# A convolution, router and experts kernel: tiles 2 and 3 on shared blocks in float32, routes ahead of rows in steps 2 to 11

## The reference

```python
out = lax.conv_general_dilated(x, weight, window_strides=(1,), padding=[(4, 4)],
                               feature_group_count=4)
y = out + einsum('nd,od->no', cond, c_weight)[:, :, None] + bias[None, :, None]
base_out = einsum('btd,od->bto', y, base_W) + base_b
probs = softmax(einsum('btd,nd->btn', y, router_W) + router_b)     # 15 routes
topk_p, topk_i = top_k(probs, 8)
w = einsum('btk,btke->bte', topk_p, onehot(expert_map[topk_i]))    # 8 experts
h = einsum('btd,erd->bter', y, A)                                  # rank 16
x = x + base_out + einsum('bter,eor->bto', h * w[..., None], B) * 2.0
```

## Time and profile before

| what | us |
|---|---|
| median of 3 runs | 185.14 |
| lowest, highest | 184.20, 185.57 |
| the profiled execution | 184.44 |
| its span in the profile | 182.6 |
| TensorE busy | 178.4 |

### The profile page before, as it was taken

How to read it: one execution, slowest core, us unless ns; L and a number is a source line. 1 busy time by engine, 2 the same in 40 slices (tenths; PEclk the granted TensorE clock), 3 DMA queues, 4 the chain that set the end, 5 groups by cost and what they waited for, 6 DMA issues and landing times.

```text
span 182.6 us, 3930 instructions
## 1 busy us (share of the span) xinstructions
PE 178.4 (98%) x1236; PEld 171.1 (94%) x1236; DVE 150.8 (83%) x509; ACT 81.2 (44%) x247; POOL 139.8 (77%) x139
## 2 busy tenths in 40 slices
PE   7999999999999999999999999999999999999993
PEld 3687999999999999999999999999999999999992
DVE  0597888898888889888888988889898889978673
ACT  3648743354544434454443445454344444422320
POOL 2118999999888898888889888888988887885620
PEclk9999999999999999999999999999999999999999
DMA  6999751757475553646565454656445721233304
GB/s 172 348 388 340 252 178 14 243 199 204 152 233 174 173 181 124 178 152 230 159 198 174 135 170 154 228 178 210 175 106 201 230 78 63 97 115 115 118 0 172
DMA packets 17876, 32.01 MB, mean 175 GB/s; under 512 B 1984, under 2 KB 3136, under 8 KB 17856
## 3 DMA queue, kind: packets, MB, share of 16 engines
q1 hardware_dynamic: 17424, 31.40, 53.1%
q10 hardware_dynamic: 432, 0.36, 0.6%
HBM read 23.36 MB, written 8.39 MB: 174 GB/s over the span
## 4 chain that ended last, share of the span: by engine, by line
PE 96%; DVE 2%; issue 0%; POOL 0%; DVEq 0%; POOLq 0%
PE wide_ps L606 62%; PE wide_ps L648 12%; PE conv_banks L592 11%; PE edge_bank L592 3%; PE conv_banks L606 2%; PE odd_bank L635 2%; PE wide_ps L554 2%; PE conv_banks L663 1%; PE conv_banks L565 1%; PE conv_banks L563 1%; DVE xr L966 1%; DVE y L856 0%; DVE y_rows L774 0%; PE edge_bank L621 0%; DVE y_hi L891 0%
## 5 line engine op out<-in xcount | busy, mean ns | idle before, releaser
L606 PE MATMUL wide_ps<-wide_hi,y_hi 128*128 128x400 f32 (+1 forms) x248 | 66.0, 326 | 0.1
L606 PE MATMUL wide_ps<-wide_hi,y_lo 128*128 128x400 f32 (+1 forms) x248 | 62.6, 313 | 0.0
L606 PE MATMUL wide_ps<-wide_lo,y_hi 128*128 128x400 f32 (+1 forms) x248 | 62.5, 313 | 0.0
L486 POOL TENSOR_TENSOR terms_lo<-terms,terms_hi 128x512 fp32r<-128x512 f32 x28 | 36.3, 1298 | 18.4 <-ACT terms_hi L385 18.4
L606 PEld LDWEIGHTS wide_ps<-wide_hi,y_hi 128*128 128x128 f32 x248 | 44.0, 188 | 2.5 <-issue 0.5
L606 PEld LDWEIGHTS wide_ps<-wide_lo,y_hi 128*128 128x128 f32 x248 | 45.9, 188 | 0.0
L606 PEld LDWEIGHTS wide_ps<-wide_hi,y_lo 128*128 128x128 f32 x248 | 45.9, 188 | 0.0
L504 POOL TENSOR_TENSOR y_lo<-y,y_hi 128x512 fp32r<-128x512 f32 x31 | 40.3, 1299 | 5.7 <-ACT y_hi L400 5.7
L481 POOL TENSOR_TENSOR xr<-xr,base_b_sb 128x512 f32<-128x512 f32 x32 | 41.7, 1302 | 0.0
L407 ACT ACTIVATE hw_hi<-odd_bank 128x128 fp32r<-128x128 f32 x31 | 8.6, 278 | 54.3 <-PE odd_bank L635 54.3
L768 DVE TENSOR_TENSOR xr<-wide_ps,xr 128x512 f32<-128x512 f32 x30 | 20.7, 691 | 5.2 <-PE wide_ps L648 3.8
(11 more groups left out here) (90 smaller groups left out, 308.4 us busy)
## 6 DMA issues: line engine op xcount, KB each, us to landing
xr<-x_rows SPq DMA_DIRECT2D x32, 256.0 KB, 3.6
out<-xr SPq DMA_DIRECT2D x31, 256.0 KB, 3.2
terms<-x_units SPq DMA_DIRECT2D x28, 256.0 KB, 2.9
...
```

The costliest lines, as they stand in the source:

```text
L486: nc.gpsimd.tensor_tensor(terms_lo[i % 2][:, :, :, :], terms[i][:, :, :, :], terms_hi[i % 2][:, :, :, :].bitcast(F32), ALU.subtract)\
L606: mm = nc.tensor.matmul(sums_of(t, k)[:, b, 0:columns[1] - columns[0]], a[k % 2][:, r, :], w[:, r, columns[0]:columns[1]], start=r == 0 an ...
```

## The change

- Tiles 2 and 3 use the shared blocks too, in float32 and without splitting (`conv_whole`): three matmuls of 256 columns for tile 2 with its edges, two for tile 3. Their differences are made by GpSimd (tile 2 and the edges, behind all of `wide_lo`, ahead of `conv_low(1)`) and by VectorE (tile 3). Their data are `first_terms` and `first_edges` in place of `x_in2` and `x_in3`; 12 weight matrices are loaded instead of 14, in another order, and the last of them earlier.
- The condition's sums of groups 1 and 2 stand together ahead of tile 0's sums, that of group 3 between their first two pieces; the sums of tile 0 take their pieces in another order.
- In steps 2 to 11 VectorE does only the first two additions of the rows, then `hw_low`, `choose` and `best`, then the edges (`reach`, split off from `condition`), and `difference` and `turn` at the end. ScalarE has `y_high` behind `hw_high`. From step 12 (`LATE`) the order is the old one.
- TensorE waits for the rows of the tile ahead only before the edge part of a convolution.
- At step 0 GpSimd does `bias_rows` ahead of `edge_low`, at step 1 ahead of `terms_low`.

The diff, cut to what changes an order or an amount of work:

```diff
-W_OWN, W_REACH = (1, 2, 5, 6), (0, 3, 4, 7)
-W_SUM, W_QUARTERS = (8, 9, 11, 12), (10, 13)
-W_ALL = 14
+W_OWN, W_REACH, W_SUM, W_QUARTERS = (1, 2, 4, 7), (0, 3), (9, 10, 5, 8), (11, 6)
+W_ALL = 12
...
-            load_x(2)
+            load_first_terms(0)
             sync.wait_ge(wide_in[0], 16)
+            sync.dma_start(first_edges[:, :, :, :], x_edges[0]).then_inc(first_edges_in, 16)
+            load_conv(4)
+            sync.wait_ge(wide_in[1], 16)
             load_conv(3)
-            load_x(3)
+            load_first_terms(1)
...
-            bias_condition(range(1, 2), 2)
+            bias_condition(range(1, GROUPS), 3)
             conv_high(1)
             y_high(1, 1, 2)
             odd_up(START, 0)
             exponentials(0, 0)
-            bias_condition(range(2, GROUPS), 3)
...
-                if up_to_tile(t, TILES - 2):
+                if from_tile(t, LATE) and up_to_tile(t, TILES - 2):
                     y_high(t + 1, k + 1)
                 if t == TILES - 1:
                     exponentials(t, k)
                 hw_high(t - 1, k - 1)
+                if not from_tile(t, LATE):
+                    y_high(t + 1, k + 1)
...
             conv_low(0)
+            pool.wait_ge(wide_lo_ready, RUNS)
+            pool.wait_ge(first_terms_in[0], 16)
+            nc.gpsimd.tensor_tensor(first_terms[0][:, 0, :, :], first_terms[0][:, 0, :, :],
+                                    first_terms[0][:, 1, :, :], ALU.subtract)\
+                .then_inc(first_difference[0], 1)
+            pool.wait_ge(first_edges_in, 16)
+            nc.gpsimd.tensor_tensor(first_edges[:, 0, :, :], first_edges[:, 0, :, :],
+                                    first_edges[:, 1, :, :], ALU.subtract)\
+                .then_inc(first_edge_ready, 1)
             conv_low(1)
             y_low(1, 1, 2)
...
-                    edge_low(p + 2, k // 2)
                     pool.wait_ge(base_b_in, 16)
                     bias_rows(t, k)
+                    edge_low(p + 2, k // 2)
                     y_low(t + 2, k + 2)
                     return
                 if t == 1:
+                    bias_rows(t, k)
                     terms_low(t + 4, k)
-                    bias_rows(t, k)
...
-                if t == START:
-                    pe.wait_ge(y_rows_ready, t - 1)
-                    pe.wait_ge(cond_biased, GROUPS)
-                elif h == 0:
-                    pe.wait_ge(y_rows_ready, t)
-                else:
-                    pe.wait_ge(y_rows_ready, t - 1)
+                pe.wait_ge(y_rows_ready, t - 1)
                 if h == 0:
                     parts.append((edge_ps, S_QUARTERS[g // 2], edge_hi, edge_lo))
                 if t < 2 * START and h == 0:
                     pe.wait_ge(conv_lo_ready, 2 + g // 2 * 2)
                 for n, (sums, j, hi, lo) in enumerate(parts):
                     if n == 2:
+                        pe.wait_ge(y_rows_ready, t)
                         pe.wait_ge(edge_lo_ready, p - START // 2 + 1)
...
-            def conv_later(t):
+            cond_sums(range(1, GROUPS - 1), 2)
+            def conv_whole(t):
+                i, h = t - FIRST, t % 2
                 pe.wait_ge(y_rows_ready, t - 1)
-                pe.wait_ge(conv_w_in[2], 16)
-                pe.wait_ge(x_loaded[t], 16)
-                conv_first(t)
+                pe.wait_ge(conv_w_in[2 + i], 16)
+                pe.wait_ge(first_terms_in[i], 16)
+                nc.tensor.matmul(conv_ps[:, h, 0, :, :], conv_sb[:, W_SUM[t], :],
+                                 first_terms[i][:, 1, :, :], start=True, stop=True)
+                pe.wait_ge(first_difference[i], 1)
+                mm = nc.tensor.matmul(conv_ps[:, h, 1, :, :], conv_sb[:, W_OWN[t], :],
+                                      first_terms[i][:, 0, :, :], start=True, stop=True)
+                if h == 0:
+                    pe.wait_ge(cond_biased, GROUPS)
+                    pe.wait_ge(first_edge_ready, 1)
+                    mm = nc.tensor.matmul(edge_ps, conv_sb[:, W_QUARTERS[t // 2], :],
+                                          first_edges[:, 0, :, :], start=True, stop=True)
+                mm.then_inc(conv_done, 1)
             def first_step():
                 runs = range(RUNS)
-                pe.wait_ge(y_hi_first, 1)
-                for r in runs:
+                def high(r):
                     pe.wait_ge(wide_hi_ready, r + 1)
                     linear(0, 0, (r,), products=(HIGH,))
-                    if r == 1:
-                        pe.wait_ge(y_lo_first, 1)
-                        linear(0, 0, range(2), products=(Y_REST,))
-                    elif r > 1:
-                        linear(0, 0, (r,), products=(Y_REST,), last=(RUNS - 1, W_REST))
-                for r in runs[:RUNS // 2]:
+                def y_rest(r):
+                    linear(0, 0, (r,), products=(Y_REST,))
+                def w_rest(r):
                     pe.wait_ge(wide_lo_ready, r + 1)
                     linear(0, 0, (r,), products=(W_REST,))
-                cond_sums(range(2, GROUPS), 2)
+                pe.wait_ge(y_hi_first, 1)
+                high(0)
+                cond_sums(range(GROUPS - 1, GROUPS), 2)
+                high(1)
+                pe.wait_ge(y_lo_first, 1)
+                y_rest(0)
+                y_rest(1)
+                high(2)
+                y_rest(2)
+                w_rest(0)
+                high(3)
+                linear(0, 0, (3,), products=(Y_REST,), last=(RUNS - 1, W_REST))
+                w_rest(1)
+                w_rest(2)
                 pe.wait_ge(wide_lo_ready, RUNS)
                 for bank, done in ((FRONT_BANK, front_done), (NEXT_BANK, linear_done)):
-                    linear(0, 0, runs[RUNS // 2:], (bank,), (W_REST,), (RUNS - 1, W_REST))\
+                    linear(0, 0, runs[RUNS - 1:], (bank,), (W_REST,), (RUNS - 1, W_REST))\
                         .then_inc(done, 1)
-                conv_later(2)
+                conv_whole(2)
...
+            def reach(t, g):
+                h = g % 2
+                shared = 1 - h
+                rows = y_rows[h]
+                reached = slice(EDGE, P) if h == 0 else slice(0, EDGE)
+                dve.wait_ge(own_ready, t - FIRST + 1)
                 nc.vector.tensor_tensor(rows[reached, :, shared, :], edge_ps[reached],
                                         rows[reached, :, shared, :], ALU.add)\
                     .then_inc(y_rows_ready, 1)
...
-            difference(START, 0)
             dve.wait_ge(top_ready, 1)
             mark(0, 0)
+            dve.wait_ge(first_terms_in[1], 16)
+            nc.vector.tensor_tensor(first_terms[1][:, 0, :, :], first_terms[1][:, 0, :, :],
+                                    first_terms[1][:, 1, :, :], ALU.subtract)\
+                .then_inc(first_difference[1], 1)
+            difference(START, 0)
             dve.wait_ge(is_expert_ready, 1)
             weigh(0, 0)
             dve.wait_ge(cond_biased, GROUPS)
             def step(t, k, p, q):
                 if t == 0:
-                    condition_first(2)
+                    condition(2, 2, 0)
+                    reach(2, 2)
                     turn(2, 2)
+                    hw_low(0, 0)
                     choose(1, 1)
                     dve.wait_ge(logits_ready, 2)
                     best(1, 1)
+                    condition(3, 3, 0)
+                    reach(3, 3)
+                    return
+                if t == 1:
+                    add_out(0, 0)
                     dve.wait_ge(top_ready, 2)
                     mark(1, 1)
-                    condition_first(3)
-                    hw_low(0, 0)
-                    return
-                if t == 1:
+                    difference(START + 1, 1)
+                    weigh(1, 1)
                     turn(3, 3)
-                    difference(START + 1, 1)
-                    add_out(0, 0)
-                    weigh(1, 1)
                     return
                 if up_to_tile(t, TILES - 3):
                     condition(t + 2, (k + 2) % GROUPS, q + (k + 2) // GROUPS)
-                    turn(t + 2, k + 2)
-                    hw_low(t - 1, k - 1)
-                elif t == TILES - 2:
+                    if from_tile(t, LATE):
+                        reach(t + 2, (k + 2) % GROUPS)
+                        turn(t + 2, k + 2)
+                if up_to_tile(t, TILES - 2):
                     hw_low(t - 1, k - 1)
                 if t == TILES - 1:
                 if t == TILES:
                     hw_low(t - 1, k - 1)
                     return
-                if up_to_tile(t, TILES - 2):
-                    choose(t, k)
-                    dve.wait_ge(logits_ready, t + 1)
-                    if up_to_tile(t, TILES - 5):
-                        difference(t + 4, k)
-                    best(t, k)
-                    dve.wait_ge(top_ready, t + 1)
-                    if up_to_tile(t, TILES - 3):
```

(19 more changed lines are left out.)

49 lines of the change are left out of this document (28 added, 21 removed).

## The result

| what | before | after |
|---|---|---|
| median, us | 185.11 (22 runs) | 185.53 (22 runs) |
| ratio of after to before | | 1.0032, 95% interval 1.0018 to 1.0046 |
| the profiled execution, us | 184.44 | 185.14 |
| its span, us | 182.6 | 183.3 |

What follows compares the result with a forecast made beforehand. TensorE was taken as the bound, busy 178.4 of 182.6 us. Savings of 1.29 + 0.37 less 0.9 left 0.75, less 0.1 at step 12, taken as 0.7: from 184.79 to 184.1 us, range 183.1 to 185.5.

Steps and rivals of the forecast that it cites:

- the 0.1 for step 12: VectorE at step 12, where the old order returns: hw_lo 1.16 us later, mostly covered by time gained before, costing 0.1 us.
- TensorE bound, eight tiles in 42.47 us, nothing to gain behind 22.00: TensorE from tile 2's sums at 22.00: matmuls fill 5.31 us a tile, so gains must come from an earlier start.
- Tiles 2 and 3 cost 1.29 less, tile 2's convolution starts 0.37 earlier: TensorE at the start: five matmuls take 2.15 us against 3.44; tile 2's convolution starts at 12.70.
- GpSimd late next: Start, ahead of tile 2's sums: TensorE waits for GpSimd's up_lo and edge_lo, giving back 0.9 us and leaving 0.75.
- It and three matmuls end at 19.98: TensorE at the start: the up projection, startable at 18.92, and three matmuls end at 19.98.
- the 0.2 that I had for the wait of the edge part: TensorE ahead of tile 2's sums: the edge part waits for GpSimd's edge_lo, ready at 20.85, costing another 0.2 us.
- Rival 1: VectorE's tile 3 difference and GpSimd collide, GpSimd gives way by 0.4 us: 0.3 saving left, 184.5 us; chance 0.22.
- Rival 2: VectorE's tile 3 difference waits until GpSimd's y_lo(1) ends at 15.7: slower by 0.4 to 0.9, 185.4 us; chance 0.10.
- by then some 0.2 x 9 has been gained: VectorE before step 12: its step takes 5.13 us against 5.31, so the lead adds up in the new order.
- Wrong if tile 2 starts before 20.9 or after 21.9, or a tile takes over 5.35 between steps 2 and 12.: Sign of failure set beforehand; tile 2's sums were expected at 21.2 to 21.4, then 42.5 us for eight tiles.

## Why the prediction was wrong

Two steps of it failed: the way from GpSimd's lateness to the start of tile 2's sums, and the 0.1 for step 12. The first is the larger.

- **TensorE bound, eight tiles in 42.47 us, nothing to gain behind 22.00.** Right for waits: tiles 2 to 11 run without one. The eight tiles took 42.59 (21.63 to 64.22), by the longer even steps.
- **Tiles 2 and 3 cost 1.29 less, tile 2's convolution starts 0.37 earlier.** The matmuls cost what I said, 0.43 to 0.44 each (starts 12.89, 13.32, 13.76), but the convolution started at 12.89, against 12.91 before by the same view, not 0.37 earlier: ScalarE's third `wide_hi` stood 1.29 for its weights, which put `high(2)` at 10.40. This was of no use or harm to the end, since the chain of after doesn't pass through TensorE between its third `wide_lo` and the up projection.
- **GpSimd late next: up(0) at 18.92, edges at 20.85. "TensorE ends at 21.25".** This step failed, by 0.63: of the 0.75, 0.12 came from the first rows to tile 2's sums. The place was right (18.99, and the edge part at 21.03), but that up(0) came so near to 18.92 is luck. My walk went from the 6.50 of before; after began 0.25 earlier, and GpSimd's chain lost 0.3 on the way, 0.2 of it beside VectorE's difference. And the step "It and three matmuls end at 19.98" took the up projection at 0.71 behind a wait. Released at 18.99, it took 0.98, and the three of the edge part 0.59 and not 0.35. A wait costs TensorE 0.25 beyond the moment of its release: the load of the weights begins only then (18.99), where in a stream a load lies under the matmul ahead (the edge part's second load at 21.11, its first matmul at 21.03). The edge part paid this though `edge_lo` was there at 20.88, for its load, due at 20.76, began at 21.00. The two make 0.5, GpSimd's chain 0.3, less the 0.2 that I had for the wait of the edge part.
- **Rival 1, the difference beside GpSimd.** It happened: right in kind, and its price on GpSimd was 0.2 and not 0.4. VectorE took 0.81 for 0.42, GpSimd 1.48 for 1.29. By the rule of the Trainium skill ("SBUF — State Buffer", Who interferes with whom) whichever is first blocks the other for its whole instruction, and the trace agrees in kind: VectorE got in about the end of `conv_lo`. GpSimd's 0.19 is less than the 0.3 that the rule would give by the starts. Rival 2 had it come behind `y_lo` and did not happen.
- **"I put 0.1 on it", step 12.** This step failed too, by 0.45. I counted "by then some 0.2 x 9 has been gained", VectorE's spare time of nine steps. In the new order it waits for `hw_hi` in every one of these steps and for the up projection in every other, so nothing is kept, and the 1.16 us that return ahead of `hw_lo` cost 0.55: 0.23 of idle time, 0.27 of restart, and a rest of 0.05. It goes with `LATE` wherever that is put: 2, 12, 20 or 29.
- **What I had no term for:** 0.2 net from a hold at a fixed place of VectorE's program, where nothing is left to spare, and 0.3 to 0.5 from addresses.
- **"Wrong if tile 2 starts before 20.9 or after 21.9, or a tile takes over 5.35 between steps 2 and 12."** The start lay inside, and would have without the luck (21.88). The odd steps take 5.5 in both kernels, so the 5.35 could only be meant for the mean of two, which was 5.32. The test looked at the stretch before the loss, and left out step 12 itself.
- **The range.** 183.1 to 185.5 missed 185.53 by a hair. Terms by what they measured, from the first rows: -0.13 at the start for the -0.75 forecast, +0.55 for the 0.1 of step 12, +0.19 and +0.35 for nothing: +0.96 for the +0.99 of turn 31.
